# Splitting 76 bank copies two to one between ACT and DVE, with new order lists, in a one-core decoder kernel

## The chip, the cores and the metric

The kernel runs on one core of one Trainium2 chip. The metric is the device time of one execution in microseconds (us); lower is better. PE is TensorE, DVE is VectorE, ACT is ScalarE, POOL is GpSimd and SP is the engine that issues most DMAs.

## The reference

Three residual blocks with a layer norm behind each run over x, 32 x 64 rows of 256 values, all in float32:

```python
x = _layernorm(x + attn(x, memory, ...))        # 8 heads, 256 memory rows, 3 retrieval steps
x = _layernorm(x + xattn(x, ctx_512, ...))      # 16 latent heads, softmax over 64 keys of each batch row
x = _layernorm(x + (x @ (weight * scale[:, None]).T + bias))
```

In the first block the normalised rows give a query per head. Each of three steps computes scores against the memory keys, turns them into weights by entmax-1.5 (the square of max(0, score/2 - threshold), with the threshold such that the weights sum to 1), and multiplies by the values. The second block is attention over a context with rotary positions. Its projections are products of several weight matrices, which depend on no row of x and can be multiplied out once. The same holds for the products of the first block.

## The kernel before, in words

**Tiles.** The 2048 rows are 16 tiles of 128 rows. Four tiles are in flight, in slots j = tile % 4. For each tile PE does, per retrieval step, `scores` in four quarters of two heads (16 matmuls, 32 instructions in the trace, L1318), then `turn_weights` in four quarters (transposes of the weights, L1329). Behind step 3 come `project` (L1341), and then the latent block and the dense block: `turn_x`, `queries` (L1365), `scores_lat` (L1376), `turn_probs`, `contexts`, `project_lat`, `turn_dense`, `dense` (L1419). A tile starts with `turn_in` (two transposes, L1301), which ACT empties in `in_out` (L752); this uses bank 4, as do the even quarters of `turn_weights` and `project`.

ACT does `spread` (scores minus a lower bound, clipped at 0, out of PSUM, L760), `resid` (the same with a threshold, L769), half of the final weights (`act_weights`, L776) and `square_weights` (squares the transposed weights out of PSUM, L781). DVE does `top` (the eight largest scores, L839), `low`, `moments` (L859), a reciprocal called `inverse` (L866), `clip`, the other half of the final weights (L879), `shift` and `sum` of the softmax, the residuals and norms. POOL does the small arithmetic of the threshold search: `limit`, `sums`, and `newton`, whose last result is `neg_u_raw` (L1038). ACT's and DVE's final weights wait for that.

**Preparation.** 76 jobs (`prep_jobs`, L254) prepare the weights, for which PE fills one PSUM bank each (`prep_job`), and another engine copies it to SBUF (`prep_out`, L630). The copy helper is L636, the scaled form L640 and L641; job 2 (`mem_t`) has a form of its own on ACT (L646). The jobs are numbered in a fixed order: 0 and 1 `wk_t`, 2 `mem_t`, 3 to 6 `k_t`, 7 to 14 `score_in`, 15 to 32 values, `score_step` and `wo_t`, 33 `ffn_t`, 34 to 53 `xwo_t`, `value_out` and `b`, 54 to 75 `kcq_t`, `wkr_t`, `n`, `m` and `a`. Jobs 72, 74 and 75 are a(2), m(3) and a(3); a(3) multiplies what the copy of m(3) left. Even jobs are copied by ACT, odd ones by DVE: 38 each. Two semaphores, one per copying engine, count the copies; who needs job x waits for count x // 2 + 1.

The load of rows 512 to 2047 of x (1.5 MB) overwrites a place that a(2) reads, so SP issues it once a(2) is filled. DVE then computes statistics of these rows in three blocks (`x_stats` 1 to 3, L488 and L903), and POOL their reciprocal roots in three groups (`x_rstd` 1 to 3, L1106 to L1117). Behind them POOL zeroes the diagonals (`diag_zero`, L1072), once all 76 jobs are filled; SP's context fetches wait for the same count. From tile 4 on the rows' `norm_in` (L834) needs these roots.

**The order of work.** Each engine works in program order. What the order is stands in a string per engine (`tile_turns`, L200). Each character names a tile (0 to f) or, as h, the preparation, and takes the next stage from that tile's stage list or from the preparation's (`tile_stages`, L147; class `Turns`). So preparation jobs stand interleaved with stages of tiles 0 to 3. Waits come with the stages; before PE writes a bank it waits for the last use of it (`bank_free`).

In this kernel's lists the following stand in the order given. POOL: x_rstd 1, 2, 3, then the last `newton` of tile 3's first step, then diag_zero. DVE: x_stats 1, 2, 3, weights of tile 2 (quarter 0), top of tile 1, `inverse` for that newton step of tile 3, two tops of tile 1, weights of tile 3. PE: the last jobs are a(2), n(3), one quarter of tile 1's turn_weights, m(3), a(3). A few stages later: tile 3's scores of step 2, turn_in of tiles 4, 6 and 5, with turn_weights of tile 2 between them; its quarter 2 stands behind turn_in of tile 5. ACT: in_out of tile 6, four quarters of tile 3's spread, in_out of tile 5. Near the middle of the run: PE has scores_lat of tile 2, turn_in of tile 11, turn_weights of tile 5; ACT has two quarters of tile 4's spread ahead of in_out of tile 11; DVE has tile 2's first shift between tile 4's low and tile 5's weights (quarter 0), and the second shift and one moments ahead of quarter 1.

Of the kernel before, what the change touches and what calls it, by code (L numbers as in the profile page):

```python
# [9 lines left out]
ACT = mybir.ActivationFunctionType  # L10
# [136 lines left out]
def tile_stages():  # L147
# [42 lines left out]
    out = [[("prep_out", x, 0, 0) for x in range(which, len(made), 2)] for which in range(2)]  # L190
    x_stats, x_rstd = ([(name, b, 0, 0) for b in range(TILES // 4)] for name in ("x_stats", "x_rstd"))
    dve_out = once("mem_norm") + out[1][:3] + x_stats[:1] + out[1][3:11] + once("ffn_scale") + out[1][11:] + x_stats[1:]
# [7 lines left out]
def tile_turns():  # L200

    return {
        "PE": "hhhhhhhhhhhhhhh0hh00001hhh1111h2hh2222hhhhhhhhhhh0hhh0hh000h0h0h0hh11h11h11hh1h1hh22hh22h2hh2hh2hh2h"
              "3hhh3333hh0h0h0h0h000h0hhh1hh11111121333334333625222272000200000444433033003038313111111155559440444"
              "4014420220222226666331313230313370777551555a555661636666161444244424142b5515555575727277772726633663"
              "664644644244433828388377477744374757553555559944949c488888888566556656666aaaad49499959965959e5868685"
              "88688a8a777577777bbbba6af67aa6aa69979799789988988888ccccb6b67bbbbb78b7aa7aaaaaa98998999998dddd7cc7cc"
              "9ccccb8b8bb8bb8bba9aa9aaaaa89eeededccd8dadd99d9d9ccaacabccbbcbbbbb9faafb9fafaebeebaeeeaeedbdddddddff"
              "fffffbfbbcbcccccccbeebeeeceeccfefcfffffdfddcddddcdccdddeceedeeeceddeddfefeeffeffddfeefeefffefeffffff",
        "DVE": "hhhhhh0hhhh00010000001h2010h1001100h110h0122102022h00h2h02h21h10h20h121211h2112011h110012h001120h202"  # L210
               "00h21020221h2022101h10h011101h0121h020h11210h3122h10212221012321032h3330h1323h1331223h310320323320h3"
               "2320h233033h2hhh213113311040050230036030330033303010303070313033010313223121223332212213121202314123"
               "4042241412112448144034140133343444302434334134344925454455532230331425345532524445353440445a34355452"
# [40 lines left out]
def prep_jobs():  # L254
# [8 lines left out]
    jobs += [("kcq_t", 0), ("wkr_t", 0), ("kcq_t", 1), ("wkr_t", 1)]  # L263
    for i in range(4):
        jobs += [("n", i)] + [("kcq_t", 2 * i + 2)] * (i < 3) + [("m", i)] + [("kcq_t", 2 * i + 3)] * (i < 3) + [("a", i)]
    return jobs


def prep_bank(x):
# [1792 lines left out]
```

## Time and profile before

| what | us |
|---|---|
| median of 3 runs (878.66 to 974.31) | 880.46 |
| the profiled execution | 881.4 |
| its span, first to last instruction | 879.5 |
| PE busy | 817.2 |
| DVE busy | 766.5 |
| ACT busy | 736.5 |
| POOL busy | 490.1 |

The span is what the trace covers, and the profiled execution's own time is 1.9 us longer. All durations in the rows come from this one execution. The mean granted clock of PE was 0.973 of full speed. In a timeline the start of the next group is the better measure of pace, since the ends of instructions overlap. An idle time in brackets is that of the engine before the group, with the instruction that ended it.

### The profile page before, as it was taken

To read this page: it belongs to the slowest core of one execution; us is meant where nothing else is said; L and a number is where in the kernel's file an instruction comes from. 1 tells how busy PE (TensorE), PEld (TensorE's weight loads), DVE (VectorE), ACT (ScalarE), POOL (GpSimd) and SP (SyncE) were. 2 spreads that over 40 slices of the span, in tenths; PEclk is the share of its full clock that TensorE was granted. 3 is DMA by queue.
4 is the path that set the end of the run, shared out by engine and by line. 5 is a ranking of instruction groups with operands and counts; after the bars stand their busy time and mean duration, and the time that the engine had idled before them with its cause. 6 is when DMAs were issued, how large, how long until landed. Compare 5 with 4: busy or idle time off the path is not lost.

```text
span 879.5 us, 18277 instructions
## 1 busy us (share of the span) xinstructions
PE 817.2 (93%) x5598; PEld 699.7 (80%) x5598; DVE 766.5 (87%) x1915; ACT 736.5 (84%) x1781; POOL 490.1 (56%) x2304
## 2 busy tenths in 40 slices
PE   6999998899999989999988999999999998999964
PEld 5878887688898878988877888888878876887852
DVE  3699998999999999989998999999989999997451
ACT  3589997999998999979899899989989899987310
POOL 4144357465655664666754666674665757566232
PEclk9999999799999989999999999999999999999986
DMA  8900002000000000000000000000000000000000
GB/s 271 226 1 1 18 20 77 9 10 5 1 1 1 1 2 0 2 16 8 15 3 1 8 1 4 2 2 1 10 19 3 7 2 1 1 8 1 1 25 16
DMA packets 24215, 17.63 MB, mean 20 GB/s; under 512 B 11760, under 2 KB 23536, under 8 KB 23856
## 3 DMA queue, kind: packets, MB, share of 16 engines
q1 hardware_dynamic: 23872, 16.13, 6.6%
q8 instruction: 48, 0.79, 0.4%
q0 software_dynamic: 240, 0.27, 0.2%
q14 instruction: 55, 0.45, 0.2%
HBM read 14.30 MB, written 2.10 MB: 19 GB/s over the span
## 4 chain that ended last, share of the span: by engine, by line
PE 65%; DVE 16%; ACT 11%; POOL 4%; issue 2%; DMA 1%; SPq 0%; POOLq 0%
PE banks L1318 26%; PE banks L1341 10%; PE banks L1329 7%; PE banks L1406 6%; PE banks L1365 5%; DVE moments L859 5%; ACT work L769 4%; DVE top L839 3%; ACT work L760 2%; PE banks L1189 2%; PE banks L1376 2%; ACT work L781 2%; PE banks L1398 2%; PE banks L1419 1%; DVE work L879 1%
## 5 line engine op out<-in xcount | busy, mean ns | idle before, releaser
L859 DVE BATCH_NORM_STATS2 moments<-work 128x6 f32<-128x512 f32 x576 | 377.1, 687 | 9.4 <-ACT work L769 6.3
L1318 PE MATMUL banks<-weights_s,work 128*128 128x256 f32 x1536 | 356.4, 385 | 1.5 <-ACT work L760 0.7
L769 ACT ACTIVATE work<-work,neg_u 128x256 f32<-128x256 f32 x768 | 332.8, 524 | 22.6 <-DVE neg_u L871 17.3
L1318 PEld LDWEIGHTS banks<-weights_s,work 128*128 128x128 f32 x1536 | 288.4, 193 | 46.5 <-issue 7.7
L760 ACT ACTIVATE work<-banks,neg_low 128x256 f32<-128x256 f32 x384 | 154.5, 499 | 5.2 <-DVE neg_low L850 4.9
L839 DVE MAX8 top<-banks 128x8 f32<-128x256 f32 x384 | 141.2, 415 | 9.6 <-PE banks L1318 8.5
L1009 POOL TENSOR_TENSOR resid_sum<-moments 128x8 f32<-128x8 f32 x144 | 30.5, 212 | 210.4 <-DVE moments L859 209.1
L1329 PE MATMUL banks<-ident,work 128*128 128x128 f32 x768 | 113.1, 283 | 20.5 <-ACT work L752 8.1
L781 ACT ACTIVATE work<-banks 128x512 f32<-128x512 f32 x192 | 113.7, 613 | 15.8 <-PE banks L1329 15.6
L1329 PEld LDWEIGHTS banks<-ident,work 128*128 128x128 f32 x768 | 90.6, 145 | 37.5 <-issue 15.8
L1341 PE MATMUL banks<-weights_s,work 128*128 128x256 f32 x512 | 115.0, 380 | 0.0
L1341 PEld LDWEIGHTS banks<-weights_s,work 128*128 128x128 f32 x512 | 95.5, 190 | 12.6 <-ACT work L781 0.2
L776 ACT ACTIVATE work<-work,neg_u_raw 128x256 f32<-128x256 f32 x192 | 85.5, 525 | 5.6 <-POOL neg_u_raw L1038 5.4
L1406 PE MATMUL banks<-latent_w,work 128*128 128x256 f32 x256 | 61.3, 395 | 3.3 <-ACT work L801 3.3
L879 DVE TENSOR_SCALAR work<-work,neg_u_raw 128x256 f32<-128x256 f32 x192 | 61.1, 367 | 3.2 <-POOL neg_u_raw L1038 2.9
L1365 PE MATMUL banks<-work,latent_w 128*128 128x128 f32 x512 | 61.4, 276 | 2.5 <-ACT work L786 2.1
L1365 PEld LDWEIGHTS banks<-work,latent_w 128*128 128x128 f32 x512 | 59.2, 192 | 4.0 <-ACT work L786 2.9
L1406 PEld LDWEIGHTS banks<-latent_w,work 128*128 128x128 f32 x256 | 50.1, 199 | 12.6 <-ACT work L801 5.6
L1093 POOL TENSOR_TENSOR work<-work 128x512 f32<-128x512 f32 x30 | 31.3, 1048 | 28.3 <-DVE work L957 28.2
L1034 POOL TENSOR_TENSOR delta<-step_num,step_inv 128x8 f32<-128x8 f32 x144 | 29.4, 206 | 31.5 <-DVE step_inv L866 30.1
L866 DVE RECIPROCAL step_inv<-step_den 128x8 f32<-128x8 f32 x144 | 27.2, 191 | 10.1 <-POOL step_den L1025 8.5
L1019 POOL TENSOR_TENSOR step_base<-sq_sum,step_sum 128x8 f32<-128x8 f32 x144 | 29.4, 204 | 11.3
(159 smaller groups left out, 1079.1 us busy)
## 6 DMA issues: line engine op xcount, KB each, us to landing
work<-in_L_xattn_Wo_dram SPq DMA_DIRECT2D x2, 1024.0 KB, 11.2
out_dram<-work SPq DMA_DIRECT2D x16, 128.0 KB, 1.8
work<-in_L_xattn_w_kc_q_dram SPq DMA_DIRECT2D x2, 768.0 KB, 5.8
rows<-in_L_xattn_Wq_dram SPq DMA_DIRECT2D x1, 1536.0 KB, 14.3
rows<-in_x_dram SPq DMA_DIRECT2D x1, 1536.0 KB, 6.6
work<-in_L_attn_Wq_dram SPq DMA_DIRECT2D x1, 1024.0 KB, 9.2
work<-in_L_attn_Wo_dram SPq DMA_DIRECT2D x1, 1024.0 KB, 12.1
work<-in_ctx_dram SPq DMA_DIRECT2D x32, 32.0 KB, 2.2
```

The source lines that it names most:

```text
L760: ins = nc.scalar.activation(q_resid0[:, j, h, :], ps_scores[:, h, :], ACT.Relu, bias=neg_low[:, j, h:h + 1])
L769: ins = nc.scalar.activation(q_resid[:, j, h, :], q_resid0[:, j, h, :], ACT.Relu, bias=small["neg_u"][:, j, h:h + 1])
L776: ins = nc.scalar.activation(q_resid[:, j, h, :], q_resid0[:, j, h, :], ACT.Relu, bias=small["neg_u_raw"][:, j, h:h + 1])
L781: nc.scalar.activation(q_weights_t[:, j, 2 * q:2 * q + 2, :], pq_turn_flat[q % 2] .rearrange("p (h n) -> p h n", h=2), ACT.Square).then_in ...
L839: ins = nc.vector.max(top[:, j, h, :], ps_scores[:, h, :])
L859: ins = nc.vector.bn_stats(moments[:, j, 2 * q:2 * q + 2, :].rearrange("p h k -> p (h k)"), r.rearrange("p h n -> p n h"))
L879: ins = nc.vector.tensor_scalar(q_resid[:, j, h, :], q_resid0[:, j, h, :], small["neg_u_raw"][:, j, h:h + 1], 0.0, ALU.add, ALU.max)
L1318: ins = nc.tensor.matmul(ps_scores[:, h, :], lhsT, w[:, h, t, :], start=(t == 0), stop=(t == CT - 1))
L1329: ins = nc.tensor.transpose(pq_turn[q % 2][:, 2 * (h % 2) + t, :], q_resid[:, j, h, P * t:P * (t + 1)], ident[:, :])
L1341: ins = nc.tensor.matmul(pq_turn_flat[0][:, 0:HID], q_weights_t[:, j, h, P * t:P * (t + 1)], value_out_w[:, h, t, :], start=(h == 0 and t ...
L1365: ins = nc.tensor.matmul(pq_pairs[:, g, :], latent_q_w[:, t, P * g:P * (g + 1)], q_row_t[:, j, t, :], start=(t == 0), stop=(t == CT - 1))
L1406: ins = nc.tensor.matmul(pq_row, q_lat_c_t[:, g, :], latent_o_w[:, g, :], start=(g == 0), stop=(g == PAIRS - 1))
```

## The change

Copies of jobs 1, 4, 7, ... (x % 3 == 1) go to DVE and all others to ACT: 25 and 51. The semaphore counts follow. The strings of all five engines are new. The number of entries of PE, POOL and SP is the same, ACT has 13 more and DVE 13 fewer, and all stages other than the copies are the same; what differs is the order.

```diff
@@ tile_stages
-    out = [[("prep_out", x, 0, 0) for x in range(which, len(made), 2)] for which in range(2)]
+    out = [[("prep_out", x, 0, 0) for x in range(len(made)) if prep_on_dve(x) == which] for which in (False, True)]
...
-    dve_out = once("mem_norm") + out[1][:3] + x_stats[:1] + out[1][3:11] + once("ffn_scale") + out[1][11:] + x_stats[1:]
+    dve_out = once("mem_norm") + out[1][:2] + x_stats[:1] + out[1][2:7] + once("ffn_scale") + out[1][7:] + x_stats[1:]
@@ tile_turns
...
-        "POOL": "hh000001100212211112200022010111102220131332233232hhh3h000000333100331112232231102211444343433440120"
+        "POOL": "hh000000101122211112200022001111010222313312233232h3hhh000010033131010332232312103211424444333440012"
...
-        "SP": "04216357109238ba4d7cfe6589dcbaef",
+        "SP": "04125391608273c5a4bed769f8bdcaef",
@@ after prep_jobs
+def prep_on_dve(x):
+    return x % 3 == 1
+
+
+def prep_outs(x):
+
+    return sum(prep_on_dve(y) == prep_on_dve(x) for y in range(x + 1))
@@ emptied_of
-                eng.wait_ge(prep_emptied[x % 2], x // 2 + 1)
+                eng.wait_ge(prep_emptied[prep_on_dve(x)], prep_outs(x))
@@ prep_out
-                    return nc.vector.tensor_copy(dst, src) if x % 2 else nc.scalar.activation(dst, src, ACT.Copy)
+                    return nc.vector.tensor_copy(dst, src) if prep_on_dve(x) else nc.scalar.activation(dst, src, ACT.Copy)
...
-                    if x % 2:
+                    if prep_on_dve(x):
...
-                ins.then_inc(prep_emptied[x % 2], 1)
+                ins.then_inc(prep_emptied[prep_on_dve(x)], 1)
@@ bank_free
-                            pe.wait_ge(prep_emptied[s % 2], s // 2 + 1)
+                            pe.wait_ge(prep_emptied[prep_on_dve(s)], prep_outs(s))
@@ queries (PE)
-                            for x in range(2):
-                                pe.wait_ge(prep_emptied[x], (N_PREP + 1 - x) // 2)
+                            for which in (False, True):
+                                done = sum(prep_on_dve(x) == which for x in range(N_PREP))
+                                pe.wait_ge(prep_emptied[which], done)
```

The strings are long. Decoded, the places that matter here read as follows in the new lists. POOL: x_rstd 1, the last newton of tile 3's first step, x_rstd 2, x_rstd 3, diag_zero. DVE: x_stats 1, the inverse for it, x_stats 2, 3, weights of tile 2 (quarter 0), two tops of tile 1, weights of tile 3; 24 copies stand ahead of x_stats 1, where 37 did. PE: a(2) stands before quarters 2 and 3 of tile 0's scores of step 3, where it stood behind them; between m(3) and a(3) stand two quarters of tile 1's turn_weights and one of its scores, and one more turn_weights quarter of tile 1 has moved from behind a(3) to ahead of m(3). The turn_ins come as 4, 6, 5, and turn_weights of tile 2 (quarters 1 to 3) now stand ahead of turn_in 5. ACT: in_out of tile 6 behind three quarters of tile 3's spread. Near the middle: PE has turn_in of tile 11, scores_lat of tile 2, turn_weights of tile 5; ACT has in_out of tile 11 ahead of tile 4's spread; DVE has both of tile 5's weights ahead of tile 2's shifts. Each list ends with the same stages of tile 15 as before.

## Rows read from the trace of the kernel before

**Rows 1.** Page, part 1: busy time in us, share of the span, instructions.

```profile
PE 817.2 (93%) x5598; PEld 699.7 (80%) x5598; DVE 766.5 (87%) x1915; ACT 736.5 (84%) x1781; POOL 490.1 (56%) x2304
```

**Rows 2.** Stretches: busy us by engine, then granted clock, DMA share, GB/s.

```profile
40.00:140.00 100.00, 96.78 (x608) 81.22 (x606) 94.58 (x227) 93.00 (x227) 42.16 (x233) 1.00 0.09 29
...
180.00:840.00 660.00, 634.63 (x4541) 548.35 (x4540) 603.03 (x1508) 590.20 (x1434) 397.77 (x1859) 0.99 0.02 5
840.00:879.50 39.50, 20.62 (x159) 14.79 (x157) 14.17 (x33) 4.47 (x9) 12.59 (x46) 0.75 0.07 23
```

**Rows 3.** Timeline of PE, 100 to 185 us: start, duration, instructions, [idle before, releaser].

```profile
109.91 7.17 PE L1318 MATMUL banks<-weights_s,work 128*128 128x256 f32 x32
116.92 0.60 PE L1249 MATMUL banks<-ident,work 128*96 128x128 f32 x4
...
137.45 1.97 PE L1189 MATMUL banks<-work 128*128 128x64 f32 x16 [1.00 <-ACT work L636]
...
148.13 1.89 PE L1318 MATMUL banks<-weights_s,work 128*128 128x256 f32 x8
151.08 0.66 PE L1329 MATMUL banks<-ident,work 128*128 128x128 f32 x4 [1.06 <-DVE work L879]
152.73 2.58 PE L1329 MATMUL banks<-ident,work 128*128 128x128 f32 x12 [0.99 <-DVE work L879]
155.09 2.65 PE L1318 MATMUL banks<-weights_s,work 128*128 128x256 f32 x8
...
168.35 1.94 PE L1329 MATMUL banks<-ident,work 128*128 128x128 f32 x8 [3.60 <-ACT work L752]
```

**Rows 4.** Groups of bank copies on DVE, 0 to 170 us: count, busy, mean ns.

```profile
L636 DVE COPY latent_w<-banks 128x512 f32<-128x512 f32 x8 | 5.4, 681 | 4.5 <-PE banks L1189 4.5
```

**Rows 5.** The same group on ACT, 0 to 170 us.

```profile
L636 ACT ACTIVATE latent_w<-banks 128x512 f32<-128x512 f32 x8 | 4.8, 604 | 4.7 <-PE banks L1189 4.7
```

**Rows 6.** Timeline of ACT, 44 to 130 us: one copy and its follower.

```profile
97.84 0.57 ACT L636 ACTIVATE work<-banks 96x512 f32<-96x512 f32 x1
98.31 0.58 ACT L781 ACTIVATE work<-banks 128x512 f32<-128x512 f32 x1
```

**Rows 7.** Timeline of POOL, 132 to 182 us.

```profile
144.99 0.20 POOL L1106 TENSOR_TENSOR tile_var<-tile_mv,eps_col 128x4 f32<-128x4 f32 x1
...
149.90 0.20 POOL L1034 TENSOR_TENSOR delta<-step_num,step_inv 128x8 f32<-128x8 f32 x1
150.18 0.20 POOL L1038 TENSOR_TENSOR neg_u_raw<-neg_u,delta 128x8 f32<-128x8 f32 x1
```

**Rows 8.** Timeline of DVE, 120 to 165 us.

```profile
147.00 0.18 DVE L866 RECIPROCAL step_inv<-step_den 128x8 f32<-128x8 f32 x1
...
150.41 2.26 DVE L879 TENSOR_SCALAR work<-work,neg_u_raw 128x256 f32<-128x256 f32 x4 [1.75 <-POOL neg_u_raw L1038]
```

**Rows 9.** Timeline of ACT, 130 to 182 us.

```profile
148.33 0.60 ACT L781 ACTIVATE work<-banks 128x512 f32<-128x512 f32 x1 [2.17 <-PE banks L1329]
...
164.49 3.03 ACT L760 ACTIVATE work<-banks,neg_low 128x256 f32<-128x256 f32 x8 [0.29 <-DVE neg_low L850]
```

**Rows 10.** Two short stretches, columns as in rows 2.

```profile
150.00:155.00 5.00, 2.95 (x17) 2.37 (x17) 4.52 (x11) 3.71 (x9) 4.12 (x13) 0.82 0.03 7
...
325.00:330.00 5.00, 5.00 (x19) 4.35 (x18) 3.84 (x10) 3.66 (x9) 2.52 (x14) 0.50 0.01 3
```

**Rows 11.** Timeline of PE, 300 to 336 us.

```profile
319.90 0.44 PE L1301 MATMUL banks<-ident,work 128*128 128x128 f32 x2
322.55 0.63 PE L1329 MATMUL banks<-ident,work 128*128 128x128 f32 x4 [2.21 <-ACT work L752]
324.67 1.12 PE L1329 MATMUL banks<-ident,work 128*128 128x128 f32 x4 [1.50 <-DVE work L879]
325.58 1.91 PE L1419 MATMUL banks<-ffn_wt,work 128*128 128x256 f32 x4
...
329.00 6.19 PE L1318 MATMUL banks<-weights_s,work 128*128 128x256 f32 x24
```

More of the change, by code:

```diff
@@ L202, in tile_turns @@
     return {
[L203 to L209, printed above, removed]
@@ L240, in tile_turns @@
-        "SP": "04216357109238ba4d7cfe6589dcbaef",
+        "PE": "hhhhhhhhhhhhhh0hh000h01hhh11121hhh2222hhhhhhhhhhh0hh0h0hhh000h0h0hh11h111h1h1hhh1h2h2h2h22h2h2h2hhh3"
+              "hh3333hhh0hh0hhh00hh00h00h11h111h1121333333343622225272200000000444403030330338313111111155559044044"
+              "4441420220222226666331313323303177057755555a55166163666616414424442414b25555557557771277272726336636"
+              "664644644424433828388377477774437457553555559944949c4888888858665656666465aaaad99495999569595e688685"
+              "8868a8a7877577777bbbb6a6af7aaa6a69977997989988988888cccc6bb6bb7bb78b7b7aa8a8aaaa9a99999998ddd7d7cccc"
+              "c9cccb8b88bb8bbbba9aa9aaaa8a9eeeedd8ccaddddd99d9cc9caacabcbbcbbbbbaf9af9bfafaeebbeeeaeaeeddbddddddff"
+              "ffffffbbbcbccccccbcbeeeeeceececffcfffffdfddcdddcdcdcdddceedeeeceeddeddfefeeffeffdfdeefeefffefeffffff",
@@ new lines, in tile_turns @@
+        "ACT": "hhhhhhhhh0hh10000hh000201111000hh0h2h22h2hh0h0hh01h1h1102hh20111102h211h0110h002122h200h100h22h2h112"
+               "1102h0021h11h10h2h3222h1110012h33h32h3h2200hh3330302222h333311h11002h0011323233131311h00040333632000"
+               "2035323307010300333222201113322221011313040443431180214411443333124444233304294445354545022013203032"
+               "234454452554445435353563366613424466015656151664657677575a446616655556773176751551564647655575474627"
+               "5125b44554456726574667742454575626257662424474666737367644367747745435475256733766763357758587788564"
+               "6684783485755865588547488776764468486c49998897866879959967768659889986795475589898daaaa9978995aaa56a"
+               "885858a7aeaa8888696598a98a9a776a777888987969988889996abbbb98678a8669bf9a89ab79a7a9b89b8a878a8aab8bb9"
+               "b99a7a9baab6bbccbc97c99879ba7cc7cca99a9a9bbbba99cacc9c99bababa9b8a8ccaab7ab8accdbdbcd8cd9bbab8b8cc8c"
+               "8acaaddbddbcacacacadadddbc9acc89bcbbd9dcddccceee9debadb9b9b9e9edbbdbbeadcadebcbbbdbdadebadcecaea9cec"
+               "bdadeaeffdfcfeedccbfafbefefdddcdefefffeddecccffffdbcdbfdfdeeeebcbffbbcfcfecceeefffcfbeedeedddfeffcef"
+               "ddddcfcfffeefcfeedddcddeeecefcfdffececeedfffdfedceeeedfdeffdfdddeffefffedefeeffefffff",
```

47 lines of the change are left out of this document (18 added, 29 removed).

## Prediction

> **What bounds the kernel now.** I read the page's busy shares first, then the table of stretches, and then PE's timeline for its real pace and its gaps. The shares say that three engines are nearly full: PE 93% of the span, DVE 87%, ACT 84% [rows 1]. The table says that it is so in every stretch but the last. While the banks are prepared beside the first tiles (40 to 140 us) PE is busy 96.8 of 100 us, DVE 94.6 and ACT 93.0; from 180 to 840 us it is 635, 603 and 590 of 660 [rows 2]. So PE's idle time is 3.2 us in the first of these and 25.4 us in the second. In the last 39.5 us PE is busy only 20.6, which is the dependent chain of tile 15 [rows 2]; all lists end with the same entries there as before, so I give it nothing.
>
> A busy PE could be a stretched one, so I check its pace: 32 score instructions from 109.91 take 7.01 us until the next group starts, 0.219 us each [rows 3]. That is full pace, and the granted clock of the stretch is 1.00, the 2.4 GHz level [rows 2]. In preparation PE sets the time, and DVE and ACT follow with about 5 and 7 us of slack in 100. The Trainium skill, "Perfetto Trace Analysis", section "Identifying the Most-Contended Engine", calls matmul busy time a bad measure, since matmuls are pipelined, and wants the weight-load share. That share is 81% in this stretch [rows 2], by which DVE and not PE would be the bound; the pace of the rows speaks against it, and its outcome is rival B.
>
> **The change, part by part.**
>
> *The copies.* DVE had 38 of 76 and has 25; ACT had 38 and has 51. In the lists, 28 of ACT's copies (jobs 20 to 74) fall between 40 and 140 us; of jobs 20 to 75 it now has 38, so 10 more there. A 128x512 copy takes 681 ns on DVE [rows 4] and 604 on ACT [rows 5], but the next ACT instruction starts 0.47 us after the copy's start [rows 6], the ends overlapping. So ACT gains 10 x 0.48 = 4.8 us of work in a stretch in which it was idle 7.0 us [rows 2]: it fits, with 2.2 us left. DVE loses at most 10 x 0.68 = 6.8 us. As PE is the bound, the relief by itself pays only through PE's idle time. The crowding costs between 0 (it all fits) and 4.8 us (none does). PE idles 3.2 us there, 1.0 of it on one ACT copy that is treated below [rows 3]; I let the other 2.2 grow by nearly half, **+1.0**. The cover is ACT's idle time; once it is used up, each further 0.48 us goes to PE.
>
> *The last banks.* The two jobs a(2) and a(3) move on PE. a(2), whose filling releases the load of the remaining rows of x, now stands before two quarters of tile 0's scores instead of behind them, so the load starts up to 3.5 us earlier (8 x 0.219 us each). DVE's statistics of x have 24 copies ahead of them instead of 37. a(3), which waited 1.00 us for ACT's copy of m(3) [rows 3], now has three other quarters between it and m(3), so this wait goes: **-1.0**. Its bank is full some 2 to 3 us later, which holds up the zeroing of the diagonals on POOL and the fetches of the context. POOL is busy with the x roots until 149.90 [rows 7], behind which the zeroing stands, so that is covered.
>
> *POOL's order after the load.* This is the clearest gain, and it is in the new lists, not in the split. Before, POOL did three groups of x roots and only then the last Newton step of tile 3: the second group starts at 144.99, the step at 149.90, and the threshold comes at 150.18 [rows 7]. DVE waited 1.75 us for it [rows 8] and ACT stood idle 2.17 us just before, waiting for PE [rows 9]. PE waited 1.06 and 0.99 us for DVE's weights [rows 3], and its clock in 150 to 155 was 0.82 on average [rows 10], so partly at the 1.2 GHz level. The new list has the step behind the first group. Its inverse, on DVE at 147.00 before [rows 8], now comes right behind the first block of x statistics, so it can be there. The threshold would come near 145.3, 4.9 us earlier. DVE's weights then start behind the three entries that its list has ahead of them (weights of tile 2, two maxima of tile 1), near 148, before PE wants them. That saves PE's 2.05 us. The slow clock goes with it: 12 transposes took 2.36 us from start to start against 1.31 at half of 0.219 each (they have 128 columns, not 256), and 8 score instructions lasted 2.65 against 1.89 [rows 3], 1.8 us together. Sum **-3.8**; the bounds are 0 (another release is late instead) and -3.8. DVE, ACT and PE all lose idle time here, so the gain isn't taken back by whichever is second.
>
> *The next gap.* At 168.35 PE resumes after 3.60 us, waiting for ACT to empty a transpose bank (in_out, L752) [rows 3]. ACT reached it after four quarters of tile 3's spread, 3.03 us from 164.49 [rows 9]. In the new lists PE needs only the in_out of tile 6, which stands after three of these quarters: 3.03 / 4 = 0.76, so **-0.8**. The rest of the gap stays.
>
> *The steady part.* All lists are replanned, by small moves: the entries of PE's move by less than one place on average, and by 10 at most. PE's costliest gap there is at 320 us: 2.21 us for ACT's in_out of tile 11 and 1.50 for DVE's weights of tile 5, and then slow matmuls [rows 11]. The clock in 325 to 330 was 0.50, the 1.2 GHz level [rows 10], after PE had stood idle 3.7 of 5 us. The slow part costs: from 324.67 to 329.00 PE took 4.33 us for work worth half, 2.2 lost, and 24 score instructions 6.19 against 24/32 of 7.17, 0.8 lost [rows 3, 11]. Together 3.7 + 3.0 = 6.7 us. In the new lists the in_out of tile 11 stands ahead of tile 4's spread on ACT, the weights ahead of the two shifts on DVE, and PE has tile 2's latent scores to do in between. All of it could go. But I can't check every other place by hand, and where 25.4 us of gaps lie scattered a replanned order opens new ones as it closes old ones. Between 0 and -6.7, and new gaps on the other side, I take **-1.0**.
>
> *The clock.* Each longer gap was followed by slow matmuls, about 0.8 us lost per us of gap (3.0 behind 3.7). The Trainium skill, "TensorE: Matmul & The Clock Gate", section "What's actually happening", says the same: the slow state is the default, and activity releases it. The rows agree, and it makes every new gap nearly twice as dear.
>
> **The sum.** The profiled execution took 881.4 us (span 879.5 and 1.9 around it). 881.4 + 1.0 - 1.0 - 3.8 - 0.8 - 1.0 = 875.8. The median of the runs is 880.46, 0.9 below the profiled one, so about **875**.
>
> **The rivals.**
> A. *ACT becomes the bound of the preparation* (slower). Place: 40 to 140 us, ACT's queue. All 4.8 us go to PE, ACT is late at the hand-over, so no gain is had there, and one more gap as at 320 costs 3.0 us of clock: 881.4 + 4.8 + 3.0 = 889.2, or 888 for the median. For it: ACT is left 2.2 us in 100, and much of what it idles is waiting that it can't fill. Against: part of that waiting is for DVE, which is relieved. It decides from the point where ACT's idle time is below 1 us and PE's above 6.
> B. *DVE was the bound.* The relief of up to 6.8 us would show in full, on top of 1.0 + 3.8 + 0.8: 881.4 - 12.4 = 869.0, 868 for the median. Against it PE's pace and its 3.2 us of idle time, which can't give 6.8.
> C. *The gap at 320 goes for good* and nothing comes for it: 5.7 us below the forecast, 869.
> D. *The change does nothing for the end*: the hand-over is 5 us earlier, but a new gap with its slow clock costs 3 + 2.4 us later: 880 to 881.
>
> **How the numbers follow.** Forecast 0.37, A 0.18, B 0.08, C 0.12, D 0.25. The forecast's own range is 871 to 879 (the hand-over saving half of its 3.8 us, or the gap at 320 giving 4 us more). The whole range reaches from B and C, a little under them, to A: 866 to 888. More than 2% from the median before (below 862.9, above 898.1), about what a measurement of this kernel can tell from no change, needs several of these at once: faster 0.03, same 0.94, slower 0.03.
>
> **What would show it.** In 40 to 140 us ACT busy near 98 and DVE near 89, PE still near 97 at 0.22 us per score instruction. No wait of PE before a(3). On POOL tile 3's threshold stands between the first and second group of x roots, and PE's idle pair near 151 to 153 is gone; the stretch 140 to 180 has less idle time and a clock above 0.84. In the steady part PE's idle time stays near 25 us, in other places. The forecast is wrong if PE idles more than 6 us in 40 to 140 on ACT's copies or spreads, if the threshold of tile 3 is no earlier, or if steady idle time changes by over 8 us.

## The result: 875.2 us, and the profile after

| what | before | after |
|---|---|---|
| median of 7 runs, us | 881.65 (878.66 to 974.31) | 875.22 (873.31 to 876.13) |
| the profiled execution, us | 881.4 | 875.46 |
| its span, us | 879.5 | 873.6 |
| mean granted clock of PE | 0.973 | 0.988 |

The ratio to before is 0.994, with the interval 0.9923 to 0.9956: by the ratio the changed kernel is 5.3 us faster (the two medians of this table lie 6.4 us apart), where 875 was forecast. Single runs far above all others, as the one of 974.31 here and one of 1214.52 among those of start_before_rest_after, aren't in the ratios. The number is right. Several of the steps that led to it are not, as the runs show.

The busy times of the kernel after (page, part 1, as in [rows 1]):

```profile
PE 809.3 (93%) x5598; PEld 691.1 (79%) x5598; DVE 760.2 (87%) x1902; ACT 741.5 (85%) x1794; POOL 493.4 (56%) x2304
```

PE has the same 5598 instructions in 7.9 us less busy time, and its idle time has grown, from 62.3 to 64.3 us (span minus busy). So the 5.9 us of span between these two traces come from matmuls that ran at full speed where they ran slowly before, and not from less idle time.

The table of stretches of the kernel after (columns as in [rows 2]):

```profile
40.00:140.00 100.00, 95.02 (x591) 79.57 (x590) 91.31 (x221) 96.75 (x236) 42.27 (x234) 1.00 0.08 26
140.00:180.00 40.00, 32.72 (x177) 27.28 (x176) 35.09 (x102) 35.20 (x89) 28.93 (x123) 0.96 0.05 11
180.00:840.00 660.00, 632.84 (x4562) 545.12 (x4563) 604.81 (x1507) 589.00 (x1433) 402.11 (x1865) 1.00 0.02 5
840.00:873.60 33.60, 16.05 (x132) 11.24 (x131) 11.93 (x28) 3.82 (x7) 8.57 (x30) 0.73 0.07 22
```

While the banks are prepared, PE is less busy than before: 95.0 instead of 96.8 [rows 2], with 17 instructions fewer in these 100 us. ACT rose from 93.0 to 96.8, DVE fell from 94.6 to 91.3. From 180 to 840 us PE idles 27.2 us where it was 25.4, but the clock is 1.00.

The timeline of PE after, 100 to 185 us (columns as in [rows 3]):

```profile
136.13 1.15 PE L1198 MATMUL banks<-work 96*64 96x128 f32 x16
...
139.74 0.68 PE L1198 MATMUL banks<-work 128*128 128x128 f32 x4 [1.44 <-DVE work L645]
...
152.02 1.12 PE L1338 MATMUL banks<-ident,work 128*128 128x128 f32 x8 [0.34 <-ACT work L790]
153.20 5.42 PE L1327 MATMUL banks<-weights_s,work 128*128 128x256 f32 x24
...
165.49 0.95 PE L1338 MATMUL banks<-ident,work 128*128 128x128 f32 x4 [3.47 <-ACT work L761]
...
178.28 0.63 PE L1338 MATMUL banks<-ident,work 128*128 128x128 f32 x4 [0.88 <-ACT work L790]
180.00 0.63 PE L1338 MATMUL banks<-ident,work 128*128 128x128 f32 x4 [1.09 <-ACT work L790]
```

All lines of code have moved down by 9 from the helper functions on. The job n(3) starts at 136.13. In the kernel before it started here (timeline of PE before, 132 to 143 us):

```profile
133.99 1.15 PE L1189 MATMUL banks<-work 96*64 96x128 f32 x16
```

So the preparation ends 2.1 us later. The wait of 1.00 us before a(3) is gone [rows 3], but one of 1.44 us has come before m(3), for a copy on DVE. The idle pair near 151 to 153 is gone: the transposes at 152.02 wait only 0.34, and tile 3's scores start at 153.20 instead of 155.09 [rows 3]. The next gap is 3.47 us, hardly less than 3.60. And two waits of 0.88 and 1.09 us for ACT's squared weights have come at 178 and 180 us.

What released tile 3's threshold is on POOL (timeline after, 140 to 152 us):

```profile
144.00 0.20 POOL L1126 TENSOR_TENSOR tile_rstd<-x_guess,x_fix 128x4 f32<-128x4 f32 x1
144.15 0.20 POOL L1043 TENSOR_TENSOR delta<-step_num,step_inv 128x8 f32<-128x8 f32 x1
144.43 0.20 POOL L1047 TENSOR_TENSOR neg_u_raw<-neg_u,delta 128x8 f32<-128x8 f32 x1
...
145.32 0.20 POOL L1115 TENSOR_TENSOR tile_var<-tile_mv,eps_col 128x4 f32<-128x4 f32 x1
```

The threshold starts right behind the first group of x roots, at 144.43 instead of 150.18 [rows 7]; the second group follows at 145.32. All 25 of DVE's copies stand ahead of x_stats 1 in the new lists, and all 38 did in the old ones, one more each than was said ahead of the prediction. On DVE (timeline after, 130 to 165 us) it has come in time for the weights of tile 3, which wait no longer, against 1.75 us before [rows 8]. The first of the two rows is the copy that m(3) waits for:

```profile
139.22 0.37 DVE L645 COPY work<-banks 128x256 f32<-128x256 f32 x1
...
147.63 1.12 DVE L888 TENSOR_SCALAR work<-work,neg_u_raw 128x256 f32<-128x256 f32 x4
```

These four instructions take 1.12 us here, where the same four took 2.26 [rows 8]. In the kernel before they ran beside the zeroing of the diagonals on POOL (timeline of POOL before, 132 to 182 us):

```profile
151.04 0.95 POOL L1072 MEMSET work<- 128x1024 f32 x1
```

The third of them lasted 1.19 us and the fourth 0.62, where 0.35 is the usual duration. Of the 192 such instructions of that trace 8 last over 0.5 us, and each of the 8 overlaps wide POOL work (the memset, or an instruction of 0.4 to 1.1 us). PE's second wait, 0.99 us, was for the fourth. So the late threshold cost DVE's weights twice, by its time and by putting them beside the zeroing. With the new order they are done before it starts, at 150.20. No run moves the zeroing alone.

The timeline of PE after, 314 to 340 us, answers to [rows 11]:

```profile
318.73 0.38 PE L1310 MATMUL banks<-ident,work 128*128 128x128 f32 x2
319.22 1.16 PE L1386 MATMUL banks<-work 64*64 64x64 f32 x64
320.71 1.06 PE L1338 MATMUL banks<-ident,work 128*128 128x128 f32 x8 [0.33 <-ACT work L761]
322.65 1.12 PE L1338 MATMUL banks<-ident,work 128*128 128x128 f32 x8 [0.89 <-ACT work L790]
323.61 3.62 PE L1327 MATMUL banks<-weights_s,work 128*128 128x256 f32 x16
```

The waits of 2.21 and 1.50 us are 0.33 and 0.89 now, and the scores behind them run at full pace: 16 instructions in 3.62 us. Three short stretches after (columns as in [rows 2]):

```profile
150.00:155.00 5.00, 4.60 (x28) 3.78 (x27) 3.63 (x8) 3.72 (x10) 3.86 (x12) 1.00 0.08 18
165.00:170.00 5.00, 4.24 (x16) 3.50 (x17) 4.98 (x13) 5.00 (x13) 3.52 (x21) 0.66 0.00 0
325.00:330.00 5.00, 5.00 (x27) 4.41 (x26) 4.94 (x14) 5.00 (x13) 2.68 (x14) 1.00 0.01 3
```

The clock in 150 to 155 rose from 0.82 and in 325 to 330 from 0.50 to the full 2.4 GHz [rows 10]. It is still low behind the gap that stayed, 0.66 in 165 to 170.

**Where the time went.** For the rest I compared when PE's same entries stand in two traces. The table gives, in us, how much later than in the trace of before they run (the median over 25 entries of PE; negative is earlier). It is worked out from the traces, and its experiments are explained below. Two things limit it. The start differs between executions: start_before_rest_after has the lists of before up to 195 us, and yet stands 1.2 us late from 33 us on. And all rows lean on the one trace of before, which lost some 3 us near 465 and 740 us that most others did not lose (last section).

```
before's time         33    106    169    202    293    327    419    484    602    824
after               0.18   1.95  -1.35  -0.48   0.30  -4.50  -3.51  -7.01  -3.09  -5.57
split_alone         0.98   4.51   3.84   3.84   3.89   2.95   2.95   1.32   1.36   0.01
pool_order_alone   -0.38  -0.33  -3.22  -3.23  -3.15  -3.74  -3.73  -5.34  -5.30  -6.59
gap320_mended      -0.60  -0.55  -0.26  -0.26  -0.22  -2.78  -2.77  -4.40  -4.36  -5.64
after_pool_undone   0.18   1.88   1.79   2.66   3.37  -1.46  -0.52  -4.13  -0.31  -2.96
```

Read the first row from left to right. The preparation loses about 2 us. The hand-over (from the last bank jobs to the tiles alone, some 130 to 170 us) gains 3.3 by these medians, and at the entry behind the gap of 3.47 us PE is 2.9 us early (165.49 against 168.35). But by 293 us it is 0.3 us late again. The gap at 320 gives 4.8 us at one place, of which 3.8 are left at 419, and what follows goes up and down.

### The profile page after: what moved, and what is told of

It is laid out like the page before. It is cut to its first block, busy times and chain, and to the rows that moved or that the text cites. A ratio compares the mean times of both kernels' runs of the same rounds, so it can differ in the third digit from the quotient of the medians.

```text
span 873.6 us, 18275 instructions
## 1 busy us (share of the span) xinstructions
PE 809.3 (93%) x5598; PEld 691.1 (79%) x5598; DVE 760.2 (87%) x1902; ACT 741.5 (85%) x1794; POOL 493.4 (56%) x2304
## 4 chain that ended last, share of the span: by engine, by line
PE 49%; ACT 25%; DVE 17%; POOL 5%; issue 2%; DMA 1%; SPq 0%; POOLq 0%
PE banks L1327 19%; ACT work L778 11%; PE banks L1350 8%; DVE moments L868 7%; ACT work L769 5%; PE banks L1416 5%; PE banks L1338 4%; PE banks L1375 4%; PE banks L1198 3%; ACT work L790 3%; DVE top L848 3%; ACT work L785 2%; DVE work L888 1%; PE banks L1386 1%; PE banks L1408 1%
## 5 line engine op out<-in xcount | busy, mean ns | idle before, releaser
L1327 PEld LDWEIGHTS banks<-weights_s,work 128*128 128x128 f32 x1536 | 284.6, 190 | 45.1 <-issue 6.2
L769 ACT ACTIVATE work<-banks,neg_low 128x256 f32<-128x256 f32 x384 | 156.4, 500 | 3.1 <-DVE neg_low L859 2.9
L1338 PE MATMUL banks<-ident,work 128*128 128x128 f32 x768 | 109.4, 277 | 18.7 <-ACT work L790 10.3
L1338 PEld LDWEIGHTS banks<-ident,work 128*128 128x128 f32 x768 | 87.4, 141 | 36.0 <-issue 21.2
L1350 PEld LDWEIGHTS banks<-weights_s,work 128*128 128x128 f32 x512 | 95.1, 190 | 13.5 <-ACT work L790 1.2
L1025 POOL TENSOR_TENSOR sq_sum<-sum_mean,moments 128x8 f32<-128x8 f32 x144 | 30.4, 211 | 11.3
```

Of the source, the lines that this page charges most:

```text
L769: ins = nc.scalar.activation(q_resid0[:, j, h, :], ps_scores[:, h, :], ACT.Relu, bias=neg_low[:, j, h:h + 1])
L1327: ins = nc.tensor.matmul(ps_scores[:, h, :], lhsT, w[:, h, t, :], start=(t == 0), stop=(t == CT - 1))
L1338: ins = nc.tensor.transpose(pq_turn[q % 2][:, 2 * (h % 2) + t, :], q_resid[:, j, h, P * t:P * (t + 1)], ident[:, :])
L1350: ins = nc.tensor.matmul(pq_turn_flat[0][:, 0:HID], q_weights_t[:, j, h, P * t:P * (t + 1)], value_out_w[:, h, t, :], start=(h == 0 and t ...
```

## The experiments

Ratios are to the kernel before, run on the same chip, with the 95% interval. A ratio's interval is 0.0013 to 0.0021 to either side, 1.1 to 1.8 us, so terms of one microsecond are at the edge of what these runs can tell. The ratio of the changed kernel (0.994) comes from the runs of the result, not from runs beside the experiments. The kernels that keep the even split use the change's code with `return x % 2 == 1`.

### The split alone, and the lists alone

split_alone: the code of the change, the order of before; the 13 moved copies stand in ACT's list where they began on DVE in the trace.

```diff
 def prep_on_dve(x):
-    return x % 2 == 1
+    return x % 3 == 1
```

> The kernel before with its own order of all tile stages; only who copies each bank is as in the change (25 on DVE, 51 on ACT), each moved copy standing in the other engine's list where it began in the trace of before. Theory 1 (PE sets the time of the preparation, the split by itself only crowds ACT): 0 to 3 us slower than before, ratio 1.000 to 1.003, PE idle in 40 to 140 us up by 1 to 3 us. Rival (DVE was the bound, its relief is the gain of the change): 3 to 6 us faster, ratio 0.993 to 0.997.

Measured: 882.91 us against 879.45, ratio 1.0036 (1.0019 to 1.0053). With the copies at these places, the split alone costs 3.2 us, a little over the 0 to 3 expected for an ACT that is only crowded. The stretch 40 to 140 us of it (columns as in [rows 2]):

```profile
40.00:140.00 100.00, 95.65 (x588) 79.13 (x586) 88.16 (x212) 93.92 (x227) 39.47 (x219) 1.00 0.05 15
```

DVE is relieved, from 94.6 to 88.2, and PE does less in the same time, 588 instructions instead of 608. So DVE was not the bound (rival B), but neither is ACT full at 93.9. PE's waits between 20 and 140 us, by what ended them (total, times, longest):

```profile
PE banks L1227 <- ACT work L645: 1.0, 2, 0.6
PE banks L1338 <- ACT work L790: 0.9, 2, 0.5
```

The loss shows as such short waits, for single copies and for the stages behind them on ACT. The rows don't add up to all of it.

lists_alone: the new order with the even split; 13 copies go back to DVE, placed by their times.

```diff
 def prep_on_dve(x):
-    return x % 3 == 1
+    return x % 2 == 1
```

> The changed kernel with its new order of all tile stages, but even banks copied by ACT and odd ones by DVE as before; each copy that goes back stands where it began in the trace of after. Theory 1 (the new lists are the gain, the split is a small cost): as fast as the changed kernel or up to 3 us faster, ratio to before 0.990 to 0.994. Rival (the split is the gain): the ratio goes back to 0.998 to 1.002.

Measured: 880.77 against 879.45, ratio 1.0011 (0.9995 to 1.0026). That lies in the range of the rival, that the split is the gain. But this run doesn't test what it was meant to: PE was 4.7 us late before the hand-over was reached, behind my own placement of the copies (its longest wait was 1.2 us for one of them on DVE). The lists and the split are planned for each other, and taking one without the other measures the misfit. The same caution holds for split_alone, whose copies I placed too. Still, the gap at 320 closed here too: from 6.06 us late to 1.30. The runs that keep the start or the rest whole, below, decide against the rival: one with the even split is as fast as the changed kernel.

### Is it ACT's load, or single copies?

If ACT's sum of work sets the price of the split, a more uneven split costs more, and one towards DVE costs other things. split_sixth leaves 13 copies on DVE and 63 on ACT, split_to_dve gives DVE two of three; both keep the order of before.

```diff
-    return x % 3 == 1
+    return x % 6 == 1     # split_sixth
+    return x % 3 != 2     # split_to_dve
```

> The kernel before with its own order of tile stages, but only every sixth bank (x % 6 == 1, 13 in all) copied by DVE and 63 by ACT, placed as in split_alone. 19 more ACT copies than before fall into 40 to 140 us, 9.1 us of work against 7.0 us of idle time. Theory A (ACT's time is the price, about 0.48 us for each copy beyond its idle time): 6 to 9 us slower than before, ratio 1.007 to 1.010, ACT busy 98 or more of 100. Theory L (the price is the wait of single copies behind longer pieces of ACT's work, not its sum): 3 to 5 us slower, ratio 1.003 to 1.006, ACT well below 98.

> The mirror image of split_alone: DVE copies two banks of three (x % 3 != 2) and ACT every third, in the order of tile stages of the kernel before. DVE was idle 5.4 us in 40 to 140 and gets about 10 copies of 0.59 us more. If both engines are as close behind PE as the idle times say: 2 to 6 us slower than before, ratio 1.002 to 1.007, so that the even split was near its best place for these lists. If DVE has room: ratio 0.999 to 1.001.

Measured: 883.9 (ratio 1.0042, 1.0021 to 1.0062) and 884.23 (1.0056, 1.0036 to 1.0077). The stretch 40 to 140 us of split_sixth:

```profile
40.00:140.00 100.00, 94.98 (x588) 79.30 (x587) 84.05 (x203) 97.53 (x236) 39.40 (x219) 1.00 0.05 14
```

and of split_to_dve:

```profile
40.00:140.00 100.00, 94.81 (x582) 78.61 (x582) 95.05 (x229) 85.73 (x208) 40.05 (x219) 1.00 0.05 15
```

Twelve more copies on ACT took it from 93.9 to 97.5% and left the price where it was, 3.7 us against 3.2. Moving work the other way cost 4.9. The longest of PE's waits between 20 and 140 us is for a single late copy each time, a scaled one on ACT in split_sixth:

```profile
PE banks L1227 <- ACT weights_s L650: 1.2, 1, 1.2
```

and one on DVE in split_to_dve:

```profile
PE banks L1227 <- DVE weights_s L649: 1.0, 1, 1.0
```

So the price doesn't follow ACT's load. The waits say that it follows where in a queue the copies stand that PE needs next; no run moves such a copy alone to show it. Rival A's mechanism (ACT becomes the bound) isn't reached even with 63 copies on ACT.

### POOL's order alone

pool_order_alone: two entries moved in the lists of before, and nothing else. In DVE's, the inverse of tile 3 stands behind x_stats 1:

```diff
-               "2320h233033h2hhh213113311040050230036030330033303010303070313033010313223121223332212213121202314123"
+               "2320h233033h2h3hh21113311040050230036030330033303010303070313033010313223121223332212213121202314123"
-        "POOL": "hh000001100212211112200022010111102220131332233232hhh3h000000333100331112232231102211444343433440120"
+        "POOL": "hh000001100212211112200022010111102220131332233232h3hhh000000333100331112232231102211444343433440120"
```

> The kernel before with two entries moved: POOL's last Newton step of tile 3's first step behind x_rstd 1 instead of behind x_rstd 3, and DVE's inverse for it behind x_stats 1. Theory 1 as it stood in the forecast (the gain of the hand-over goes through to the end): 3 to 4 us faster, ratio 0.9955 to 0.9965, and PE's idle pair at 151 to 153 us gone. Rival (ACT, which comes right behind PE, takes it back within the next 30 to 50 us, as the comparison of the two traces suggests: 3.3 us ahead near 160, 0.5 near 206): ratio 0.999 to 1.001, with the tiles from 8 on starting within 1 us of before.

Measured: 876.76 against 879.45, ratio 0.9973 (0.9958 to 0.9988), 2.4 us, a little under the 3 to 4 expected. POOL of this kernel, 140 to 152 us:

```profile
144.82 0.20 POOL L1043 TENSOR_TENSOR delta<-step_num,step_inv 128x8 f32<-128x8 f32 x1
145.10 0.20 POOL L1047 TENSOR_TENSOR neg_u_raw<-neg_u,delta 128x8 f32<-128x8 f32 x1
```

The threshold comes 5.1 us earlier than in [rows 7], and PE (140 to 172 us) shows what it is worth:

```profile
150.71 1.11 PE L1338 MATMUL banks<-ident,work 128*128 128x128 f32 x8 [0.34 <-ACT work L790]
151.89 1.97 PE L1327 MATMUL banks<-weights_s,work 128*128 128x256 f32 x8
...
165.13 1.94 PE L1338 MATMUL banks<-ident,work 128*128 128x128 f32 x8 [3.44 <-ACT work L761]
```

Tile 3's scores start at 151.89 instead of 155.09. In the table of shifts PE is 0.3 us early before the hand-over, 3.2 behind it, and still 3.15 at 293 us: here nothing is given back, so the moved threshold by itself keeps what it gains. The next gap stays, 3.44 us. The threshold is 0.7 us later than in the changed kernel (144.43). There SP issues the load of the remaining rows of x at 132.72 instead of 134.09, DVE's statistics start at 139.51 instead of 140.69 (in this kernel 140.51), and no step of the forecast had priced that.

### The POOL order undone in the changed kernel

after_pool_undone:

```diff
-               "h3hh2113311100003403062300330031303031015313000317301330023322322333222213111201231442022243414111b4"
+               "hhh21313311100003403062300330031303031015313000317301330023322322333222213111201231442022243414111b4"
-        "POOL": "hh000000101122211112200022001111010222313312233232h3hhh000010033131010332232312103211424444333440012"
+        "POOL": "hh000000101122211112200022001111010222313312233232hhh3h000010033131010332232312103211424444333440012"
```

> The changed kernel with POOL's last Newton step of tile 3's first step put back behind x_rstd 3, and DVE's inverse for it back behind a top of tile 1. Theory 1 (this order is worth 2 to 4 us in either kernel): 2 to 4 us slower than the changed kernel, ratio to before 0.996 to 0.999. Rival (in the changed kernel ACT's queue takes it back before tile 8, where the trace showed it only 0.5 us ahead): ratio stays 0.993 to 0.9955.

Measured: 879.44 against 880.0, ratio 0.9984 (0.9971 to 0.9998): 3.9 us of the changed kernel's 5.3 are gone. Its PE, 145 to 165 us, waits again:

```profile
152.44 1.06 PE L1338 MATMUL banks<-ident,work 128*128 128x128 f32 x8 [1.73 <-ACT work L790]
...
155.02 5.42 PE L1327 MATMUL banks<-weights_s,work 128*128 128x256 f32 x24
```

DVE's weights stand beside the zeroing again, too (timeline of DVE, 145 to 156 us):

```profile
149.31 2.26 DVE L888 TENSOR_SCALAR work<-work,neg_u_raw 128x256 f32<-128x256 f32 x4 [1.69 <-POOL neg_u_raw L1047]
```

### The gap at 320 alone

gap320_mended: in the lists of before, turn_in of tile 11 ahead of tile 2's latent scores on PE, in_out of tile 11 ahead of tile 4's spread on ACT, and both of tile 5's weights ahead of tile 2's shifts on DVE. PE's and DVE's lines:

```diff
-               "4014420220222226666331313230313370777551555a555661636666161444244424142b5515555575727277772726633663"
+               "4014420220222226666331313230313370777551555a55566163666616144424442414b25515555575727277772726633663"
-               "6567665456557167454774425245444176664645756267525546444667464776464774462777755447375532475757766675"
+               "6567665456557167454774455224444176664645756267525546444667464776464774462777755447375532475757766675"
```

> The kernel before with four entries moved near 320 us: ACT empties tile 11's turn_in ahead of tile 4's spread, DVE does both quarters of tile 5's weights ahead of tile 2's shifts, PE has tile 11's turn_in ahead of tile 2's latent scores. Theory 2 (the changed kernel got most of its time here, from PE's 3.7 us gap and the 3.0 us of slow clock behind it): 4 to 6.7 us faster, ratio 0.992 to 0.9955. Rival (DVE and ACT are as late as before, another gap takes its place): within 1 us, ratio 0.999 to 1.001.

Measured: 878.68 against 879.45, ratio 0.998 (0.9964 to 0.9996), 1.8 us, where 4 to 6.7 were expected if the gap was most of the gain, and under 1 if another took its place. It lies between. Its PE, 314 to 340 us:

```profile
318.59 1.16 PE L1386 MATMUL banks<-work 64*64 64x64 f32 x64
320.87 1.07 PE L1338 MATMUL banks<-ident,work 128*128 128x128 f32 x8 [1.12 <-DVE work L888]
323.55 1.88 PE L1429 MATMUL banks<-ffn_wt,work 128*128 128x256 f32 x4 [1.61 <-DVE work L958]
325.22 1.94 PE L1338 MATMUL banks<-ident,work 128*128 128x128 f32 x8
```

The wait for ACT is gone, but DVE's shift, pushed back, now delays PE by 1.61 us, and the transposes at 325.22 still run slowly (1.94 us for what took 1.06 to 1.12 above). At this place 2.6 us are gained, in the changed kernel 4.8. Its PE has 32 score instructions and more between these transposes and the dense block, which may be why; no run shows it alone.

### Start of one kernel, rest of the other

In these three kernels the lists up to 195 us are those of one kernel and the rest has the order of the other.

start_before_rest_after: start of before with its even split, rest of after.

> All lists of the kernel before up to 195 us of its trace (so the even and odd split, and POOL's old order at the hand-over), and from there the order of the changed kernel. Theory 1 (the rest of the new lists is what pays, the start of the change nets about 0): 4 to 6 us faster than before, ratio 0.993 to 0.9955. Rival (the gain is made of both parts, or of lists fitted to the split): 0 to 2 us faster, ratio 0.998 to 1.000.

start_before_pool_rest_after: the same with the two entries of pool_order_alone moved as well.

> As the run above, with POOL's last Newton step of tile 3's first step behind x_rstd 1 and DVE's inverse for it behind x_stats 1. Theory 1 (hand-over gain and the rest of the lists add up, the split is not needed): 7 to 9 us faster than before, ratio 0.990 to 0.992, so faster than the changed kernel. Rival (the two take the same gap): ratio 0.993 to 0.996.

start_after_rest_before: start of after with its split, rest of before.

> All lists of the changed kernel, split included, up to 195 us of its trace, and from there the order of the kernel before. Theory 1 (the preparation loses 2 us to the split, the hand-over gives 3 and some is lost on ACT until 200 us): 0 to 1 us faster than before, ratio 0.999 to 1.000. Rival (the start carries the gain): ratio 0.994 to 0.996.

| kernel | us (before: 880.0) | ratio | interval |
|---|---|---|---|
| start_before_rest_after | 878.27 | 0.9977 | 0.9962 to 0.9992 |
| start_before_pool_rest_after | 875.77 | 0.9942 | 0.9924 to 0.9961 |
| start_after_rest_before | 878.13 | 0.9979 | 0.9966 to 0.9992 |

The first is close to its rival's range and the third lies between its two. The rest of the new lists is worth 2.0 us, about what the gap at 320 alone gave. With POOL's order added it is 5.1 us, as much as the whole change, though this kernel has the even split and the old order in the preparation. That is less than the 7 to 9 us expected, since the rest gave 2.0 and not 4 to 6: its ratio is in the rival's range, but the two parts add up (2.0 and 3.1) and don't take the same gap. And the new start by itself (1.8 us) gives no more than POOL's order alone (2.4). So the two-to-one split isn't what makes the changed kernel faster. With fitted lists neither a cost nor a gain of it shows; the runs would tell one of more than about 2 us.

### Attempts at a better version

after_in_out: the changed kernel waited 3.47 us at 165.49 for in_out of tile 6. This entry is moved ahead of all quarters of tile 3's spread on ACT, and with it the squared weights of tile 2 (step 2, quarter 1), which stood behind the fourth:

```diff
-               "1102h0021h11h10h2h3222h1110012h33h32h3h2200hh3330302222h333311h11002h0011323233131311h00040333632000"
+               "1102h0021h11h10h2h3222h1110012h33h32h3h2200hh3330302222h333311h11002h0011323233131311h00040623333000"
```

> The changed kernel with two entries of ACT moved near 162 us: in_out of tile 6 and the squares of tile 2 (step 2, quarter 1) stand ahead of all four quarters of tile 3's spread instead of behind three and four. Theory 1 (the gap of 3.5 us before tile 2's transposes and the slow clock behind it are a loss of the order alone): the gap falls to about 1 us, the clock in 165 to 170 stays near 1, and the kernel is 2 to 4 us faster than the changed one, ratio to before 0.989 to 0.992. Rival (DVE, which gets tile 3's spread 1.3 us later, takes it back): ratio 0.993 to 0.995.

Measured: 876.3 against 879.5, ratio 0.9959 (0.9943 to 0.9975), no better than the changed kernel and above both ranges expected. Its PE, 155 to 200 us:

```profile
162.68 1.11 PE L1338 MATMUL banks<-ident,work 128*128 128x128 f32 x8 [0.65 <-ACT work L761]
163.88 1.97 PE L1327 MATMUL banks<-weights_s,work 128*128 128x256 f32 x8
...
169.70 0.66 PE L1310 MATMUL banks<-ident,work 128*128 128x128 f32 x2 [3.85 <-ACT work L790]
```

The gap fell from 3.47 to 0.65 us, and one of 3.85 came 6 us later, also for ACT. In the changed kernel ACT works without a break in 165 to 170 (5.00 of 5 us, above); in this one it waits 0.65 us for DVE's step on tile 3 at 166.57, which is the rival's mechanism in part. Moving these ACT entries ahead only chose which of PE's entries waits.

after_all_mends: this, and three more such moves: n(3)'s copy four places earlier on DVE, and on ACT two squared weights of tile 9 and one copy of tile 11's probabilities one to three places earlier. DVE's line:

```diff
-               "h20102121h211001h10101210100h121212213h02h21021023132123330113h32332h2312311332h3203022323203033302h"
+               "h20102121h211001h10101210100h121212213h02h21021023132123330113h32332h2312311332h320302232320303h3302"
```

> As the run above, with four more entries moved: DVE copies bank n(3) two entries earlier (PE waits 1.44 us for it near 138 us), ACT squares tile 9's first two quarters one to three entries earlier (1.6 us near 455), and ACT copies tile 11's second half of the probabilities ahead of a quarter of tile 12's weights (1.6 us near 732). Theory 1 (each gap taken away is kept in part): 1 to 3 us below the run above, ratio to before 0.986 to 0.990. Rival (ACT and DVE are as full as PE, moves only shift the gaps): equal to the run above within 1 us.

Measured: 876.98 against 879.5, ratio 0.9966 (0.9951 to 0.9982), equal to the run above within 1 us, as the rival had it. Its PE, 134 to 172 us:

```profile
138.78 0.71 PE L1198 MATMUL banks<-work 128*128 128x128 f32 x4 [1.31 <-ACT latent_w L645]
...
168.83 0.66 PE L1310 MATMUL banks<-ident,work 128*128 128x128 f32 x2 [3.86 <-ACT work L790]
```

With n(3)'s copy earlier on DVE, m(3) waits 1.31 us for a copy on ACT instead of 1.44 for the one on DVE. The gap near 169 is the one of the run before. No version I tried beats the changed kernel; start_before_pool_rest_after equals it.

## Why the prediction was right, and where it was not

**The pace of PE as the bound of the preparation.** Right. Neither of the two splits that take work off DVE gained anything (the third gives it more), which is what the pace in [rows 3] had said against the share of the weight loads. The Trainium skill, "Perfetto Trace Analysis", section "Optimizing Scalar/DVE Operations", says that offloading from DVE to Scalar may make sense if DVE is saturated. DVE at 94.6% is near that, and the runs show a loss of 3.2 us from the offload alone.

**Copies, +1.0.** The sign was right and the size too small. n(3) starts 2.1 us later in the changed kernel, and the split alone costs 3.2. I priced it by ACT's extra load beside PE. By the waits, what costs is single copies that stand late in a queue, whichever queue is the fuller one.

**The last banks, -1.0.** Wrong. The wait before a(3) went as forecast, but m(3) got one of 1.44 us, so that the term is +0.4 and not -1.0, since the copy that it needs is now the last of DVE's copies and stands behind moments and reductions. I looked at the wait that goes and not at the neighbour's releaser.

**POOL's order, -3.8.** Right in place and, in the main, in mechanism. I put all of PE's 2.05 us of waiting down to the late threshold; the 0.99 of it came through DVE's weights that ran beside the zeroing of the diagonals, 2.26 us for four instead of 1.12. It goes with the same two moved entries, so the sum didn't suffer. The runs give 2.4 us (in the old lists), 3.1 (start of before, rest of after) and 3.9 (undone in the changed kernel), where I took the bound of 3.8. In the timelines the hand-over from n(3) to tile 3's scores takes 17.1 us instead of 21.1. Of these 4.0 us, 1.2 come from transposes at 139 to 142 us that ran slowly before (clock 0.70 in 140 to 145), which I hadn't seen.

**The next gap, -0.8.** Wrong: it fell by 0.13. The timeline of ACT after, 160 to 172 us:

```profile
162.35 2.30 ACT L769 ACTIVATE work<-banks,neg_low 128x256 f32<-128x256 f32 x6 [0.52 <-DVE neg_low L859]
```

Three quarters of spread take 2.30 us here, against 3.03 for four [rows 9], so the 0.7 was there. But they begin 2.1 us earlier (162.35 against 164.49), waiting for DVE, and PE comes to the gap 2.7 us earlier (162.02 against 164.75, the starts less the idle times). The 0.6 between the two took the saving back. The step had held PE's arrival fixed.

**The steady part, -1.0.** Mis-sized. The gap at 320 gave 4.8 us in the profile, 3.8 by 419 us, and 1.8 alone (as a ratio), where I took 1.0 of 6.7; rival C's mechanism was there for the most part.

**What no step had.** Between 165 and 293 us the changed kernel gives back 3.2 us of PE's lead (from 2.9 early to 0.3 late), among them the waits of 0.88 and 1.09 for squared weights at 178 and 180. The new order from 195 us on has a share in it: start_before_rest_after, with the lists of before up to there, goes from 0.8 late at 169 us to 2.1 at 202 and 3.0 at 293 in the same comparison, where pool_order_alone loses nothing. That is rival D's mechanism without its consequence, since the gap at 320 then paid. Both rivals were given a chance each as whole outcomes; what happened was half of either, and together they land on the forecast. On the one side stand the costs that I undersized in the preparation (1.1 at n(3), 1.4 for the last banks), 0.7 of the next gap and the 3.2 given back. On the other stand 2.8 more than I took at 320, the 1.2 of slow transposes and the rest further on. That they cancel is luck: the number is better than the steps.

**What would show it.** DVE 91.3 and ACT 96.8 (near 89 and 98 forecast), PE 95.0 (near 97), idle 5.0, under the limit of 6. The threshold stands where it should, the clock in 140 to 180 is 0.96 against 0.84. Its idle time there isn't less, though: 7.3 us, where it was 6.9. Steady idle time is 27.2, as forecast near 25.

**What stays open.** In the profile, the lead moves between -3.1 and -7.0 us after 419 us. Part is the clock's chance (below), and for the rest no run separates the places. Nor is the price of the split in fitted lists known to better than about 2 us. And no run tells what the earlier threshold is worth by itself and what leaving the zeroing's company is.

## What to carry to other kernels

Before relieving an engine, ask whether the one it feeds runs at its full pace. Where it did, here, the relief paid nothing, and each operation moved had to find a place in a second queue that was nearly as full. Look instead for short entries in an in-order queue that stand ahead of a result for which three engines wait: here 4.9 us of roots that nobody needed yet (144.99 to 149.90) were worth 2 to 4 us, for two moved characters. Where all queues are nearly full, a gap that is closed by moving an entry can open again a few microseconds on, as it did in after_in_out, or stay closed, as behind POOL's order. So follow PE's lead to the end before counting it.

## What was unexpected of the hardware

The same order of work does not always fall into the slow clock at the same places. pool_order_alone has before's lists from 170 us on, yet gains 1.6 us near 465 and 1.3 near 740, where nothing differs. Two stretches of the kernel before (columns as in [rows 2]):

```profile
462.00:475.00 13.00, 10.82 (x59) 8.60 (x58) 11.16 (x27) 11.26 (x29) 6.79 (x35) 0.87 0.01 2
735.00:745.00 10.00, 7.36 (x41) 5.51 (x40) 9.85 (x24) 9.85 (x25) 8.47 (x37) 0.83 0.00 0
```

and of pool_order_alone:

```profile
462.00:475.00 13.00, 11.29 (x74) 9.37 (x75) 11.95 (x32) 12.23 (x33) 6.34 (x30) 1.00 0.01 2
735.00:745.00 10.00, 9.43 (x51) 8.04 (x51) 9.74 (x25) 10.00 (x26) 8.25 (x44) 1.00 0.00 0
```

The gap in front is the same in both (timelines of PE, before and pool_order_alone):

```profile
467.25 0.69 PE L1351 MATMUL banks<-ident,work 128*128 128x128 f32 x2 [2.18 <-DVE work L940]
463.54 0.44 PE L1360 MATMUL banks<-ident,work 128*128 128x128 f32 x2 [2.19 <-DVE work L949]
```

gap320_mended shows the same two gains, and the clock is 1.00 in both stretches of split_alone and split_sixth too, which also have before's order there. So the same gap can bring the 1.2 GHz level in one execution and not in another. Since only one trace of each kernel is kept, this is read across kernels; a single profile can be off by some 3 us in this way. The difference in clock between the two kernels is more than that: in its longest series (35 executions, beside split_alone) before has a mean clock of 0.974 to 0.982, in the seven executions of the result the changed kernel has 0.983 to 0.988. Between the two traces all of the gain appears as less slow time of PE, 7.9 us, with 2.0 us more idle time.

DVE and POOL are not independent either. DVE's weights instruction (one operand of 128 x 256 in SBUF) takes 0.35 us. The one that ran beside the zeroing took 1.19 to 1.24 us in all eight kernels in which the two met, from before to split_to_dve, and in none of the others did a weights instruction last that long at this place.
